# Block 4 of a fused decoder kernel: all steps behind the maxima three of sixteen ticks nearer to them

## The reference, cut to what matters

```python
q = _split_heads(query @ Wq.T + bq)          # query: layernorm(x), 8 x 100 x 256
k = _split_heads(key @ Wk.T + bk)            # key, value: the context, 8 x 361 x 256
v = _split_heads(value @ Wv.T + bv)          # 16 heads of 16
scores = jnp.einsum('bhtd,bhsd->bhts', q, k) * scale
scores = jnp.where(mask[:, None, None, :], scores, -jnp.inf)
attn = jax.nn.softmax(scores, axis=-1)
out = jnp.einsum('bhts,bhsd->bhtd', attn, v)
x = x + out @ Wo.T + bo
```

## Time and profile before

| | us |
|---|---|
| median of 3 runs | 445.34 |
| lowest and highest | 443.82, 445.56 |
| the profiled execution's own time | 443.37 |
| its span in the trace | 441.5 |
| PE busy | 407.4 (92% of the span) |
| DVE busy | 263.1 (60%) |
| ACT busy | 175.0 (40%) |
| POOL busy | 135.8 (31%) |

### The profile page before, as it was taken

The page is one execution under the profiler, slowest core; times in us unless marked ns, Lnnn a source line. Parts: engine busy times, 40 slices in busy tenths (PEclk is TensorE's granted clock), DMA queues, the critical chain, the costliest instruction groups (busy, mean ns, idle before and its releaser), DMA issues.

```text
span 441.5 us, 7539 instructions
## 1 busy us (share of the span) xinstructions
PE 407.4 (92%) x2991; PEld 267.6 (61%) x2991; DVE 263.1 (60%) x473; ACT 175.0 (40%) x360; POOL 135.8 (31%) x183
## 2 busy tenths in 40 slices
PE   6999997894999999989979999999998999999976
PEld 2556754452656677658845555567765766666644
DVE  4149558499412363002379699995397677777324
ACT  0450450000443314523246585451205666666740
POOL 3830019332474300670562000000035473310100
PEclk9899999797899998999999999999999999999999
DMA  7994003000012279643210000018645446310002
GB/s 225 393 267 135 2 0 101 0 0 0 1 51 84 68 244 378 274 129 107 67 29 0 0 1 1 0 32 185 177 128 136 121 105 154 100 44 2 3 1 76
DMA packets 32850, 42.19 MB, mean 96 GB/s; under 512 B 7712, under 2 KB 29132, under 8 KB 32418
## 3 DMA queue, kind: packets, MB, share of 16 engines
q1 hardware_dynamic: 29897, 34.18, 25.5%
q0 software_dynamic: 2304, 5.76, 5.1%
q10 hardware_dynamic: 614, 1.77, 1.9%
HBM read 33.00 MB, written 8.98 MB: 95 GB/s over the span
## 4 chain that ended last, share of the span: by engine, by line
PE 61%; DVE 20%; issue 6%; ACT 5%; POOL 5%; DMA 3%; SPq 0%; POOLq 0%; DVEq 0%; ACTq 0%
PE banks L1073 6%; PE banks L1494 5%; PE banks L1479 4%; PE banks L1374 4%; PE banks L1448 4%; PE banks L1113 4%; PE banks L1135 4%; PE banks L1102 3%; DVE RA L484 3%; DVE NM L1848 2%; PE banks L1160 2%; PE banks L1244 2%; PE banks L1262 2%; PE banks L1342 2%; PE banks L1062 2%
## 5 line engine op out<-in xcount | busy, mean ns | idle before, releaser
L1848 DVE TENSOR_REDUCE NM<-banks 100x2 f32<-100x722 f32 x64 | 56.4, 903 | 19.4 <-PE banks L1448 19.1
L1342 PE MATMUL banks<-XT,RBG 128*128 128x400 f32 x192 | 65.0, 500 | 1.6 <-ACT XT L809 1.6
L1342 PEld LDWEIGHTS banks<-XT,RBG 128*128 128x128 f32 x192 | 36.3, 190 | 29.7 <-ACT XT L809 1.2
L1021 ACT ACTIVATE CT<-banks 128x400 f32<-128x400 f32 (+1 forms) x72 | 35.8, 504 | 23.2 <-PE banks L1479 21.7
L809 ACT ACTIVATE XT<-banks 128x800 f32<-128x800 f32 x10 | 8.3, 838 | 61.6 <-PE banks L1062 61.6
L1374 PE MATMUL banks<-W,RC 128*100 128x256 f32 x128 | 30.7, 380 | 0.6 <-DVE RC L1744 0.6
L752 POOL TENSOR_TENSOR rstd<-ve,mhalf 100x2 f32<-100x2 f32 x4 | 2.8, 702 | 88.2 <-DVE ve L1816 88.2
L1606 DVE TENSOR_TENSOR RC<-RV 128x800 f32<-128x800 f32 x16 | 15.6, 1022 | 16.1 <-ACT RV L851 14.1
L1211 PE MATMUL banks<-RC,SELT 128*128 128x400 f32 x64 | 24.3, 526 | 1.0 <-DVE RC L1646 0.7
L641 POOL TENSOR_TENSOR rstd<-ve,mhalf 100x4 f32<-100x4 f32 x10 | 10.6, 1065 | 46.3 <-DVE ve L1558 46.3
L1374 PEld LDWEIGHTS banks<-W,RC 128*100 128x100 f32 x128 | 21.0, 167 | 6.2 <-DVE RC L1744 1.0
(11 more groups left out here) (244 smaller groups left out, 843.9 us busy)
## 6 DMA issues: line engine op xcount, KB each, us to landing
RA<-in_L_ffn_W SPq DMA_DIRECT2D x2, 2048.0 KB, 12.4
k_parts<-RA SPq DMA_DIRECT2D x18, 180.5 KB, 3.4
RBG<-in_L_attn_W_aiv SPq DMA_DIRECT2D x1, 3072.0 KB
CT<-in_ctx_t SPq DMA_DIRECT2D x2, 1444.0 KB, 11.4
RA<-k_parts SPq DMA_DIRECT2D x12, 180.5 KB, 3.4
RBG<-k_parts POOLq DMA_DIRECT2D x12, 180.5 KB, 4.3
RA<-k_parts POOLq DMA_DIRECT2D x12, 180.5 KB, 3.8
RBG<-in_ctx SPq DMA_DIRECT2D x2, 1024.0 KB, 17.5
```

The costliest lines, as they stand in the source:

```text
L1021: sc.activation(P4[slot][0:n, g * HG * T:(g + 1) * HG * T], PS[4 + w % 2][0:n, 0:HG * T], ACT.Exp).then_inc(st_exp, 1)
L1342: ins = mm(PS[2 * aiv_pair(j, w) + g][:, 0:GC], WA[:, k, c:c + P], XT[:, k, GC * g:GC * g + GC], start=(k == 0), stop=(k == KT - 1))
L1848: v.tensor_reduce(NM[:, b % 2, 2 * i:2 * i + 2], PP[w % 2][0:T, :, 0:S], AX.X, ALU.max, negate=True).then_inc(mx_out, 1)
```

## The change

All steps of `PLAN` but the maxima get a tick three lower, and so do those steps of `ONCE` that prepare the last pair of batches (two lower for x_add, zero_bank and ln_stats). The ticks of the fill move too; there are still five of them. No instruction is added, removed or altered, and no wait is: only the order of instructions on PE, DVE and ACT changes.

```diff
         PLAN = ([("maxima", 2 * i, i) for i in range(PAIRS)]
-                + [("parts", 21, 0)]
-                + [("scores", 28 + TICKS * u // UNITS4, u) for u in range(UNITS4)]
-                + [("weighted", max(35 + u // 2, 32 + TICKS * u // UNITS4), u) for u in range(UNITS4)]
-                + [("os_evac", 46, 0), ("sums_tr", 49, 0), ("normalise", 49, 0), ("out_tr", 56, 0),
-                   ("out_mm", 58, 0), ("add", 59, 0)])
-        PLAN_END = TICKS * (B - 1) + 60
+                + [("parts", 18, 0)]
+                + [("scores", 25 + TICKS * u // UNITS4, u) for u in range(UNITS4)]
+                + [("weighted", max(32 + u // 2, 29 + TICKS * u // UNITS4), u) for u in range(UNITS4)]
+                + [("os_evac", 43, 0), ("sums_tr", 46, 0), ("normalise", 46, 0), ("out_tr", 53, 0),
+                   ("out_mm", 55, 0), ("add", 56, 0)])
+        PLAN_END = TICKS * (B - 1) + 57
 
         ONCE = ([("mix_last", 2 * i if i < 14 else 2 * i - 11, 4 + i) for i in range(2 * RT - 4)]
                 + [("ln_norm", 15, 2), ("x_tr", 18, 2), ("x_out", 18, 2), ("q_mm", 20, 2), ("q_out", 20, 2),
-                   ("x_add", 27, 3), ("zero_bank", 28, 0), ("ln_stats", 31, 3), ("ln_norm", 36, 3),
-                   ("x_tr", 40, 3), ("x_out", 41, 3), ("q_mm", 43, 3), ("q_out", 44, 3)])
+                   ("x_add", 25, 3), ("zero_bank", 26, 0), ("ln_stats", 29, 3), ("ln_norm", 33, 3),
+                   ("x_tr", 37, 3), ("x_out", 38, 3), ("q_mm", 40, 3), ("q_out", 41, 3)])
 ...
-        FILL = (21, 23, 25, 27, 28)
+        FILL = (21, 22, 23, 24, 25)
```

## The result

| us | before | after |
|---|---|---|
| median (executions) | 445.45 (4) | 451.51 (4) |
| lowest, highest | 443.82, 445.91 | 448.82, 453.78 |
| profiled execution, its span | 443.37, 441.5 | 449.25, 447.5 |

The account below looks back on a forecast made before the run. TensorE was taken to bound block 4. Middle batches 4.5 us, the last P 1.06 and the start 1.0 summed to 6.6 us more, put on the median 445.34: 451.9 us, range 447.7 to 454.2.

Parts of the forecast that it names:

- The wait of P: Middle batches: P, the parts' transposition, may start 3.46 us after T, TensorE gets there after 2.71: 0.75 us wait each.
- The alternation: TensorE, each batch: 12 runs of fp32 work instead of 11 cost 0.15 us more, between 0 and 0.20.
- The last P: Between T of batch 5 and of 6: the transposition of batch 7's parts waits 1.06 us.
- The start: Start of block 4: T of batch 0 0.7 us late, plus 0.31: 1.0 us, bounds -0.7 and +1.6.
- the queue would let the copies go sooner: Start: SyncE's queue free at 333.17, copies before issued from 333.66; S(0,0) not delayed, cover 0.4 us.
- P waits less: Middle batches: DVE reaches M(b,7)'s reduction without `normalise` ahead; 0.38 us a batch, alternation free, 448.9 us. Chance 0.15.
- Only the start loses: From batch 2 on POOL's parts are in time and the alternation costs nothing: 446.3 us. Chance 0.10.
- the hole closes: Start of block 4: nearer scores fill 1.08 us of idle TensorE, P never waits: 443.3 to 444.3 us. Chance 0.08.
- The clock falls: Block 4: after waits at the start TensorE runs at half clock, costing 2.9 us: 454.8 us. Chance 0.05.

Follow-up runs that it names:

- the kernel with pairs: Kernel before, scores and weighted units issued two and two, out_tr, out_mm and add two ticks later than in a first paired form: 439.19 us, ratio 0.9875.
- the first pairs: Kernel before with scores and weighted units issued in pairs, five later steps moved by one or two ticks: 445.19 us, ratio 0.9983.
- the kernel after again: The changed kernel, unaltered, measured once more beside the kernel before on another chip: 452.25 us, ratio 1.0168.
- the pairs again: The second paired order of scores and weighted units, unaltered, measured once more beside the kernel before: 438.86 us, ratio 0.9862.
- POOL slowed: Changed kernel with one of POOL's four steps on the parts done four times, 0.78 us slower: 471.84 us in one execution.

## Why the prediction was right, and which of its terms were not

**The wait of P: right.** By distances of starts, P comes 3.38 us after T (401.19 - 397.81), and PE is there 2.72 us after T (400.07, and 0.46 for the second pair of W, as in the earlier trace rows). Predicted were 3.46 and 2.71: a wait of 0.66 us instead of 0.75 (the row's 0.58 is counted from the end of the last W); one batch is in fact 0.64 us longer (11.82 against 11.18). The steps: T to the reduction 1.31 (1.27 predicted), from its start to POOL's 0.96 (0.98), POOL 1.06 (1.05), the step from POOL to P 0.05 (0.16). The last was read from a P that PE reached late of itself, so it was no price of the hop.

**The alternation: the term that failed.** 0.15 us a batch was predicted and none was there: with P one tick later and no wait a batch takes 11.16 us, before 11.18. An M ahead of a W cost 0.40 us (398.91 to 399.31), which the prediction had, as 0.31 and 0.10, in the way to P. But the run that is new stands at the output transposition, of which the prediction said that no row shows it. PE of the kernel after:

```profile
391.07 0.51 PE L1448 MATMUL banks<-RA,RC 97*100 97x361 bf16 x2
391.42 0.34 PE L1517 MATMUL banks<-identf,zrow 100*128 100x100 f32 x2
391.60 0.35 PE L1479 MATMUL banks<-RC,RBG 100*105 100x100 bf16 x4
```

M and out_tr take 0.35 + 0.18 = 0.53 us here. Before, with out_tr behind the W and M after it, they took 0.23 + 0.31 = 0.54 us (starts at 389.97, 390.20 and 390.51). The run costs nothing at that place. The count of runs with a price from another pair of operations was the wrong way to cost it; the mean of 0.17 us in the kernel with pairs shows that the price is real elsewhere. This and the wait, some 0.1 us too long, make most of the 1.4 us by which the five middle batches were overestimated: 5 x 0.90 predicted, 5 x 0.62 measured.

**The last P: right.** 1.37 us predicted for T(5) to T(6) (1.06 of wait and the M of 0.31), 1.47 measured, with a wait of 1.09 in the row.

**The start: right in kind, too large.** T(0) came 0.36 us late and not 0.7. P(0) came 0.87 us behind x_tr for 0.97, which is 0.41 us of wait by distances of starts for the 0.51 predicted (0.24 in the row), and P(1) came 13.84 us after x_tr for 14.2. S(0,0) did wait, 0.34 us, which was predicted at nothing with a cover of 0.4. The step that failed there is that the queue would let the copies go sooner. SyncE's queue came to the mask row 3.14 us after x_tr (2.90 before), and the row took 1.39 us where 1.09 had been seen, so the queue was free 0.54 us later against x_tr than the prediction had it. The three copies were issued 4.57 us after x_tr (4.48 before), and S(0,0) started 3.05 us after that, as before (3.07). P(0) came some 3 us sooner than before, and its DMAs did not.

**The rivals.** P waits less: it needed DVE free of `normalise`, and the run with `normalise` one tick later got 11.46 us, so this rival was a different program. Only the start loses, and the hole closes: both needed P without a wait, and 3.9 us of waits speak against them. The clock falls: it had 0.05 as a case on its own, for the start, and that was the wrong question. It does not fall in every execution or in none. In both profiles of the kernel after P(1) waited 1.31 us and the clock held; in that with `normalise` later it fell behind the same wait. It cost 1.5 us behind P(7) in one, 2.8 in the last block in another. So the number came out right for a reason and a half. The order's cost was right in kind and forecast too high (6.6 us for 4.9 in the profiles), and the rest was made up by a clock that the forecast had at full in every execution. That the two errors cancel to 0.4 us is luck. That the medians hold such losses is an inference from the profiles, as each timed execution shows only its mean clock: 0.977 for 448.82 us, 0.962 for 453.77 us.

## What to carry to other kernels

When steps move nearer to what they wait for, write down for each wait both sides in distances from one common event (here T): what the engine has to do until it gets there, and the chain until the release; one tick of other work in between was worth 4 us here, and in the middle batches a slower POOL cost nothing in one order and its full length in the other. Cost a change of neighbours by the very pair that meets, not by the number of changes, and look for the order with fewer of them only after its waits are counted: it gave 1.3% here once the waits were out. A new wait on a full TensorE costs its own length and, in some executions, a stretch at half clock behind it.

## What was not expected of the hardware

- The same row of waits at the end of block 4 and in the last block (0.63, 0.81, 0.67, 0.99 us) goes with a full clock in five profiles (T(7) to the end near 17.0 us: before, `normalise` later, the first pairs, the kernel after again, the pairs again) and with a fall in seven (18.4 to 21.1 us). Up to the first fall PE is busy alike: 0.97 of 2.30 us after, 0.98 of 2.40 us before, both at 1.00. What decides it stays open.
- Waits of 0.58 us once per batch never brought the clock down in the profiles of the kernel after; waits of about 1.35 us once per batch did, behind two of five of them (POOL slowed). One of 2.75 us (P alone three ticks nearer) was followed by 15 us at half clock, with PE busy all the time (3.00 of 3.00 us in each of five stretches).
- A change from bf16 to fp32 matmuls and back has no one price: 0 us at the output transposition, 0.17 us in the mean of five.
